# Softmax sums inverted on 16 columns by VectorE instead of 512, the context scaled by VectorE instead of GpSimd, and the score banks' two skipped places moved, in an attention layer on one core

## The chip, the cores and the metric

The kernel runs on one core of a Trainium2 chip. The metric is the device time in microseconds (us) of one execution, the median of several.

## The reference, cut to what matters

```python
x = L0_attn_query                      # 4 x 2048 x 512, fp32
xn = layernorm(x)
q, k, v = (split_heads(xn @ w.T + b) for each of q, k, v)       # 16 heads of 32
attn = softmax(q / sqrt(32) @ k.T)                              # per head 2048 x 2048
ctx = attn @ v
x + (ctx @ out_w.T + out_b) + tanh(((xn @ weight) @ aux1) @ aux2 + bias)
```

Four batches of 16 heads make 64 heads of attention, each with 2048 queries, 2048 keys and a head size of 32.

## The kernel before, in words

Three stages follow one another: `build_weights` prepares the weights, `build_project` makes q, k, v and the feed-forward part, and `build_attend` works through the 64 heads and then multiplies by the output weights. The change touches `build_attend` (and one constant in `build_weights`). Every order below is written out by hand; semaphores join the engines.

**TensorE.** A head has 64 units, 16 tiles of 128 keys (`kt`) by 4 blocks of 512 queries. For each unit TensorE makes two matmuls alternately: `scores` of the current head into one of three banks `st_bank` (line 1031), and `max_scores` (line 1015) of a head that comes later into one of four banks `sm_bank`, from which the row maxima are taken. They run in blocks of two tiles, 8 units, 16 matmuls. Behind each block stands `use` of the two tiles before (line 1037, `pv_bank`: probabilities times v). After tiles 8 and 9 of the next head comes `add_up`: the sum over the keys of the finished head, a matmul with `ones` that leaves each sum 32 times over in its bank `sum_bank`, which is one of the four `sm_bank` places.

**ScalarE** takes the exponential of each `st_bank` (line 846), copies `pv_bank` and the sums (line 853) to SBUF, and issues seven loads for a later head after tiles 6, 7, 9, 10, 12, 13 and 15 (lines 271 and 277).

**VectorE** reduces each `sm_bank` to its maxima (line 929), in the order of the units k = 0 to 63. Into this row the 512 reciprocals of the head's sums are put as three pieces (line 921), after k = 63, 7 and 15.

**GpSimd** adds ten of the sixteen probability tiles, nine instructions of 128x2048 (line 781, called add 0 to add 8 here). The other six tiles, `CHAINS`, are added by accumulating DMAs that GpSimd issues: join 1 to join 5 (line 792), each of which waits until the one before has landed, then `merge` (line 800), which adds GpSimd's sum and releases `add_up`. Its order per head is: join 1, add 0, merge of the head before, add 1, join 2, add 2, add 3, join 3, add 4, add 5, join 4, add 6, add 7, join 5, `scale` of the head before (line 806), add 8. Join 1 also waits for TensorE to have used tile 0 of its head, since tile 0 lies in the buffer that is added to.

**SyncE** stores each scaled context (line 700) and loads the row of maxima (line 695).

How a place of the three score banks is found:

```python
def st_slot(u):

    return u + (u >= 22) + (u >= 44)
```

A unit waits for the exponential of the last unit in the same bank. That is normally the third before it. After a skipped place two units wait for the second before, and one for the fifth before. Blocks begin at units that are multiples of 8.

Of the kernel before, what the change touches and what calls it, by code (L numbers as in the profile page):

```python
# [7 lines left out]
ACT = mybir.ActivationFunctionType  # L8
ALU = mybir.AluOpType
AX = mybir.AxisListType  # L10

P = 128
# [25 lines left out]
TURN_UNIT = 8  # L38
BEGIN = 16
SUM_UNIT = 56  # L40
RECIPS = [63, 7, 15]
CUT = 10
# [9 lines left out]
SLOT = {kt: i % 7 for i, kt in enumerate([*range(1, 13), 14, 15])} | {13: 7}  # L52
SCALE_ADD = 8
RESULT_TILES = [9, 11]
# [42 lines left out]
def st_slot(u):  # L97

    return u + (u >= 22) + (u >= 44)

# [9 lines left out]

assert early_maxima(BLOCKS - 1, BLOCK_UNITS - 1)[-1] == HEAD_MAXIMA - 1 and UNITS < TURN_SLOT
assert UNITS == 64 and len(SM_TURN) % SM_BANKS == 0 and st_slot(UNITS - 1) == 65


# [12 lines left out]
def build_weights(nc, x, w, dram, keep, first):  # L127

    with ExitStack() as own:
# [41 lines left out]
        @block.gpsimd  # L171
        def _(pool):
            nc.gpsimd.memset(keep["ident"][:], 0.0).then_inc(ident_ready, 1)
            nc.gpsimd.memset(keep["ones"][:], 1.0)
            nc.gpsimd.memset(keep["power"][:], -0.5)
            pool.wait_ge(ident_ready, 1)
            nc.gpsimd.affine_select(out=keep["ident"][:], in_=keep["ident"][:], compare_op=ALU.not_equal, fill=1.0,
                                    base=0, pattern=[[-1, P]], channel_multiplier=1).then_inc(ident_ready, 1)
            pool.wait_ge(var_ready, 1)
            nc.gpsimd.tensor_tensor(keep["rstd"][:], keep["rstd"][:], keep["power"][:], ALU.pow).then_inc(rstd_ready, 1)  # L180
# [426 lines left out]
def build_attend(nc, dram, out, first):  # L607
# [3 lines left out]
    with ExitStack() as own:  # L611
# [12 lines left out]
        pv_copy = [sb(f"pv_copy{s}", [P, BLK]) for s in range(2)]  # L624
        sum_copy = [sb(f"sum_copy{s}", [P, BLK]) for s in range(2)]
        ratio = sb("ratio", [P, BLK])
# [12 lines left out]
        join_due, joined = sem("join_due"), [sem("joined0"), sem("joined1")]  # L639
        pool_added, sums_ready, recip_ready, context_ready = sem("pool_added"), sem("sums_ready"), sem("recip_ready"), sem("context_ready")  # L640
        pv_copied, sums_copied = sem("pv_copied"), sem("sums_copied")
        context_stored = [sem("context_stored0"), sem("context_stored1")]
# [123 lines left out]
        def _(pool):  # L766
            pool.sem_inc(pool_added, PRIME)
            pool.sem_inc(context_ready, PRIME)
            nc.gpsimd.memset(k_st[3][MROW:MROW + 1, :].bitcast(F32), 1.0).then_inc(consts_ready, 1)
# [31 lines left out]

            def scale(h, r):
                pool.wait_ge(pv_copied, PRIME + h + 1)
                pool.wait_ge(recip_ready, h * len(RECIPS) + len(RECIPS))
                pool.wait_ge(context_stored[r % 2], PRIME + (h // 2) * (CTX_DMAS * DMA))
                nc.gpsimd.tensor_tensor(ctx_out[r % 2][:], pv_copy[r % 2][:], ratio[:], ALU.mult).then_inc(context_ready, 1)  # L806

            def sum_up(h, r, i):
# [21 lines left out]
        def _(act):  # L830
            for s in (probs_ready, pv_copied, sums_copied):
                act.sem_inc(s, PRIME)
# [16 lines left out]

            def copy_bank(h, r, bank, copies, ready, value, copied):  # L850
                act.wait_ge(ready, value)
                act.wait_ge(context_ready, PRIME + h - 1)
                nc.scalar.activation(copies[r % 2][:], bank[:], ACT.Copy).then_inc(copied, 1)  # L853

            def copy_pv(h, r):
                copy_bank(h, r, pv_bank, pv_copy, tile_used, PRIME + h * KT + KT, pv_copied)

            def copy_sums(h, r):
                copy_bank(h, r, sum_bank, sum_copy, sums_ready, PRIME + h + 1, sums_copied)

# [19 lines left out]
            def body(h, r, more, following):  # L880
                for kt in range(CUT, KT):
                    exps(h, r, kt)
                    if kt in LOAD_AT and more >= GROUP - 1:
                        load(h + GROUP - 1, (r + GROUP - 1) % GROUP, LOAD_AT.index(kt))
                if more:
                    for kt in range(CUT):
                        exps(following, (r + 1) % GROUP, kt)
                        if kt == 1:
                            copy_pv(h, r)
                        if kt in LOAD_AT and more >= GROUP:  # L890
                            load(h + GROUP, r, LOAD_AT.index(kt))
                        if kt == CUT - 1:
                            copy_sums(h, r)
                else:
                    copy_pv(h, r)
                    high(2, 0)
                    copy_sums(h, r)

# [5 lines left out]
        def _(dve):  # L904
            dve.sem_inc(max_scores_read, PRIME + UNITS + AHEAD * PER_TILE)
            dve.sem_inc(res_ready, PRIME)
            dve.sem_inc(row_max_ready, PRIME + 1)

            def negate(s):
# [3 lines left out]

            def recip(h, r, piece):

                if piece == 0:
                    dve.wait_ge(sums_copied, PRIME + h + 1)
                    dve.wait_ge(context_ready, PRIME + h)
                cut = [BLK // len(RECIPS) // 8 * 8 * i for i in range(len(RECIPS))] + [BLK]
                columns = slice(cut[piece], cut[piece + 1])  # L920
                nc.vector.reciprocal(ratio[:, columns], sum_copy[r % 2][:, columns]).then_inc(recip_ready, 1)  # L921
# [50 lines left out]
            def body(h, r, more, following):  # L972
                if more == 0:
# [7 lines left out]
                    results(1, 1)  # L981
                    for piece in range(len(RECIPS)):
                        recip(h, r, piece)
                else:
# [13 lines left out]
        def _(pe):  # L998
# [4 lines left out]
            def max_scores(s, r, k):  # L1003
# [182 lines left out]
```

## Time and profile before

| | us |
|---|---|
| median of 3 runs | 4139.67 (4138.31 to 4141.12) |
| profiled execution, its own time | 4140.99 |
| profiled execution, span | 4139.2 |
| TensorE busy | 4072.0 |
| VectorE busy | 3125.5 |
| ScalarE busy | 2356.7 |
| GpSimd busy | 3253.4 |

The span runs from the first to the last instruction of the profiled execution. TensorE's matmuls overlap, so its busy time holds waits too; start times are the better guide. The attention stage runs from about 0.82 ms to 3.98 ms.

### The profile page before, as it was taken

How to read it: one execution, taken by the hardware profiler on the slowest of the kernel's cores; microseconds unless marked ns; L12 is line 12 of the kernel's file. 1: busy time of each engine (PE TensorE's matmuls, PEld its weight loads, DVE VectorE, ACT ScalarE, POOL GpSimd, SP SyncE). 2: the span in 40 equal slices, each digit the busy share in tenths (PEclk: the TensorE clock that was granted, in tenths of full speed). 3: DMA queues.
4: the chain of work that ended last, by engine and by line, in shares of the span. 5: the costliest groups of instructions: out<-in, count | busy, mean ns of one | idle time of the engine just before them, and what ended most of it. 6: DMA issues, size and time to landing. Idle time of an engine off the chain costs nothing.

```text
span 4139.2 us, 77715 instructions
## 1 busy us (share of the span) xinstructions
PE 4072.0 (98%) x21216; PEld 2495.7 (60%) x21216; DVE 3125.5 (76%) x5058; ACT 2356.7 (57%) x4515; POOL 3253.4 (79%) x1180
## 2 busy tenths in 40 slices
PE   8999999999999999999999999999999999999999
PEld 6888888755555555555555555555555555555467
DVE  4344334788888888888888888888888888888554
ACT  2222222266666666766666667666666766676621
POOL 1222222299999999999999999999999999999930
PEclk9999999999999999999999999999999999999999
DMA  4444445578888888888888887888888888888787
GB/s 170 158 167 162 152 147 169 161 149 175 174 178 172 174 170 175 170 173 176 176 176 172 174 170 167 175 175 175 179 169 176 172 173 172 176 176 173 156 263 262
DMA packets 246352, 722.11 MB, mean 174 GB/s; under 512 B 87392, under 2 KB 88416, under 8 KB 184544
## 3 DMA queue, kind: packets, MB, share of 16 engines
q0 software_dynamic: 55296, 402.68, 50.2%
q1 hardware_dynamic: 107648, 201.88, 14.4%
q10 hardware_dynamic: 83040, 113.01, 9.8%
q8 instruction: 185, 3.03, 0.3%
q14 instruction: 183, 1.50, 0.1%
HBM read 178.00 MB, written 136.31 MB: 76 GB/s over the span
## 4 chain that ended last, share of the span: by engine, by line
PE 46%; DMA 19%; issue 9%; POOL 3%; ACT 3%; POOLq 0%; ACTq 0%; SPq 0%; DVE 0%; DVEq 0%
PE sm_bank L1015 14%; PE pv_bank L1037 14%; PE st_bank L1031 14%; DMA dma_sum<-probs 11%; DMA dma_sum<-pool_sum 8%; ACT probs L846 3%; PE sm_bank L261 2%; POOL pool_sum L781 2%; PE sm_bank L1037 1%; PE st_bank L261 1%; POOL ctx_out L806 1%; PE sm_bank L1024 0%; POOL dma_sum L792 0%; DMA q_stack<-s_ctx 0%; ACTq L845 0%
## 5 line engine op out<-in xcount | busy, mean ns | idle before, releaser
L929 DVE TENSOR_REDUCE part_max<-sm_bank 128x1 f32<-128x512 f32 x4016 | 2442.1, 678 | 410.9 <-PE sm_bank L1015 404.1
L781 POOL TENSOR_TENSOR pool_sum<-pool_sum,probs 128x2048 f32<-128x2048 f32 x512 | 2504.8, 4892 | 16.6 <-ACT probs L846 0.7
L846 ACT ACTIVATE probs<-st_bank 128x512 f32<-128x512 f32 x3840 | 1959.8, 616 | 611.9 <-PE st_bank L1031 585.5
L1031 PE MATMUL st_bank<-q_stack,k_stack 97*128 97x512 f32 x4096 | 1649.2, 404 | 15.0 <-ACT probs L846 8.5
L1015 PE MATMUL sm_bank<-k_stack,q_stack 96*128 96x512 f32 x4016 | 1655.5, 412 | 5.3 <-issue 2.8
L1015 PEld LDWEIGHTS sm_bank<-k_stack,q_stack 96*128 96x128 f32 x4016 | 764.8, 190 | 551.9 <-DVE part_max L929 331.7
L1031 PEld LDWEIGHTS st_bank<-q_stack,k_stack 97*128 97x128 f32 x4096 | 780.5, 191 | 268.4 <-ACT probs L846 127.5
L1037 PE MATMUL pv_bank<-probs,v_pairs 128*32 128x512 f32 x7680 | 934.9, 602 | 0.0
L1037 PEld LDWEIGHTS pv_bank<-probs,v_pairs 128*32 128x32 f32 x7680 | 205.5, 110 | 455.7 <-ACT probs L846 262.8
L792 POOL DMA_DIRECT2D dma_sum<-probs x320 | 348.6, 1089 | 66.0 <-ACT probs L846 28.9
L405 POOL TENSOR_TENSOR y_out<-y_out,x_in 128x512 f32<-128x512 f32 x64 | 82.8, 1293 | 369.6 <-ACT y_out L437 365.2
L781 POOL TENSOR_TENSOR pool_sum<-probs 128x2048 f32<-128x2048 f32 x64 | 330.5, 5164 | 0.1
L921 DVE RECIPROCAL ratio<-sum_copy 128x168 f32<-128x168 f32 (+1 forms) x192 | 230.9, 1204 | 38.1 <-ACT sum_copy L853 38.1
L524 DVE SCALAR_TENSOR_TENSOR qk_lo<-proj,qk_bias,qk_hi 128x512 fp32r<-128x512 f32 x128 | 96.1, 751 | 195.0 <-ACT qk_hi L431 193.3
L431 ACT ACTIVATE qk_hi<-proj,qk_bias 128x512 fp32r<-128x512 f32 x128 | 88.1, 688 | 272.4 <-PE proj L261 272.4
L437 ACT ACTIVATE y_out<-y_out 128x512 f32<-128x512 f32 x64 | 40.5, 632 | 319.6 <-DVE y_out L513 319.6
L846 ACT ACTIVATE dma_sum<-st_bank 128x512 f32<-128x512 f32 x256 | 132.4, 603 | 132.4 <-PE st_bank L1031 132.3
L394 POOL TENSOR_TENSOR rstd<-rstd,power 128x4 f32<-128x4 f32 x15 | 15.3, 1017 | 190.5 <-DVE rstd L459 190.5
L513 DVE TENSOR_TENSOR y_out<-proj,row_bias 128x512 f32<-128x512 f32 x64 | 44.3, 692 | 121.8 <-PE proj L261 121.8
L853 ACT ACTIVATE sum_copy<-sm_bank 128x512 f32<-128x512 f32 x64 | 38.2, 597 | 168.9 <-PE sm_bank L1037 168.9
L502 DVE TENSOR_TENSOR v_out<-proj,row_bias 128x512 f32<-128x512 f32 x64 | 44.3, 692 | 104.7 <-PE proj L261 104.7
L806 POOL TENSOR_TENSOR ctx_out<-pv_copy,ratio 128x512 f32<-128x512 f32 x64 | 103.6, 1619 | 20.8 <-issue 20.8
(116 smaller groups left out, 3198.6 us busy)
## 6 DMA issues: line engine op xcount, KB each, us to landing
dma_sum<-probs POOLq DMA_DIRECT2D x320, 1024.0 KB, 8.3
dma_sum<-pool_sum POOLq DMA_DIRECT2D x64, 1024.0 KB, 10.2
q_stack<-s_q_hi ACTq DMA_DIRECT2D x122, 256.0 KB, 6.4
k_stack<-s_k_hi ACTq DMA_DIRECT2D x122, 256.0 KB, 4.4
x_in<-in_x SPq DMA_DIRECT2D x16, 1024.0 KB, 7.7
s_q_hi<-qk_hi SPq DMA_DIRECT2D x16, 1024.0 KB, 4.3
s_q_lo<-qk_lo SPq DMA_DIRECT2D x16, 1024.0 KB, 6.4
s_k_hi<-qk_hi SPq DMA_DIRECT2D x16, 1024.0 KB, 4.3
```

What stands on the lines that cost most here:

```text
L261: last = nc.tensor.matmul(out, a(c), b(c), start=(c == 0 and n == 0), stop=(c == CT - 1 and n == 2))
L431: nc.scalar.activation(qk_hi[:, t, g], proj[:, u % RING], ACT.Identity, bias=keep["qk_bias"][:, t, g:g + 1]).then_inc(hi_ready, 1)
L524: nc.vector.scalar_tensor_tensor(qk_lo[:, t, g], proj[:, u % RING], keep["qk_bias"][:, t, g:g + 1], qk_hi[:, t, g].bitcast(F32), ALU.add, ...
L781: nc.gpsimd.tensor_tensor(total[:], one[:], tile_at(r, kt)[:], ALU.add).then_inc(pool_added, 1)
L792: nc.gpsimd.dma_start(dma_sum[r % 2][:], tile_at(r, CHAINS[0][j])[:], accum_op=ALU.add).then_inc(joined[r % 2], DMA)
L806: nc.gpsimd.tensor_tensor(ctx_out[r % 2][:], pv_copy[r % 2][:], ratio[:], ALU.mult).then_inc(context_ready, 1)
L846: nc.scalar.activation(tile_at(r, kt)[:, q * BLK:(q + 1) * BLK], st_bank[:, st_place(kt * QB + q)], ACT.Exp, scale=SCALE).then_inc(probs_r ...
L921: nc.vector.reciprocal(ratio[:, columns], sum_copy[r % 2][:, columns]).then_inc(recip_ready, 1)
L929: nc.vector.tensor_reduce(part_max[:, k:k + 1], sm_bank[:, sm_place(k)], AX.X, ALU.max).then_inc(max_scores_read, 1)
L1015: nc.tensor.matmul(sm_bank[:, sm_place(k)], q_st[r][0:ROWS, q * P:(q + 1) * P], k_st[r][0:ROWS, b * BLK:(b + 1) * BLK], start=True, stop=T ...
L1031: nc.tensor.matmul(st_bank[:, st_place(u)], k_st[r][0:ROWS + 1, kt * P:(kt + 1) * P], q_st[r][0:ROWS + 1, q * BLK:(q + 1) * BLK], start=Tr ...
L1037: last = nc.tensor.matmul(bank[q * DH:(q + 1) * DH, :], left, right[:, q * BLK:(q + 1) * BLK], start=start, stop=stop)
```

## The change

The sums' bank is read by VectorE with a reduction that transposes blocks of 32x32: of the 32 equal rows and 32 columns of a block it leaves one column, and 512 columns become 16. The 16 columns are inverted; since each sum is added 32 times, `ones` holds 1/32. A transposing copy spreads the 16 columns to 512 again, and VectorE, not GpSimd, multiplies the context. ScalarE's copy of the sums goes away; TensorE's next use of that bank waits for VectorE instead. The skipped places are at units 24 and 48.

```diff
+ST_SKIPS = (24, 48)
-RECIPS = [63, 7, 15]
+INVERT, SPREAD, SCALED = SUM_UNIT, 63, 15
...
-    return u + (u >= 22) + (u >= 44)
+    return u + sum(u >= skip for skip in ST_SKIPS)
...
-            nc.gpsimd.memset(keep["ones"][:], 1.0)
+            nc.gpsimd.memset(keep["ones"][:], 1.0 / DH)
...
-            def scale(h, r):
-                pool.wait_ge(pv_copied, PRIME + h + 1)
-                pool.wait_ge(recip_ready, h * len(RECIPS) + len(RECIPS))
-                pool.wait_ge(context_stored[r % 2], PRIME + (h // 2) * (CTX_DMAS * DMA))
-                nc.gpsimd.tensor_tensor(ctx_out[r % 2][:], pv_copy[r % 2][:], ratio[:], ALU.mult).then_inc(context_ready, 1)
...
-                    if i == SCALE_ADD:
-                        scale(h, r)
...
-                        if kt == CUT - 1:
-                            copy_sums(h, r)
...
+            def invert(h):
+                dve.wait_ge(sums_ready, PRIME + h + 1)
+                nc.vector.tensor_reduce(totals[:], sum_bank.rearrange("p (b j) -> p b j", j=DH), AX.X, ALU.add,
+                                        apply_transpose=True).then_inc(sums_turned, 1)
+                dve.wait_ge(sums_turned, PRIME + h + 1)
+                nc.vector.reciprocal(inverse[:], totals[:]).then_inc(inverse_ready, 1)
+
+            def spread_out(h):
+                dve.wait_ge(inverse_ready, h + 1)
+                nc.vector.transpose(ratio[:].rearrange("p (b j) -> p b j", j=DH),
+                                    inverse[:].unsqueeze(2).to_broadcast([P, BLK // DH, DH])).then_inc(ratio_ready, 1)
+
+            def scale(h, r):
+                dve.wait_ge(pv_copied, PRIME + h + 1)
+                dve.wait_ge(ratio_ready, h + 1)
+                dve.wait_ge(context_stored[r % 2], PRIME + (h // 2) * (CTX_DMAS * DMA))
+                nc.vector.tensor_tensor(ctx_out[r % 2][:], pv_copy[r % 2][:], ratio[:], ALU.mult).then_inc(context_ready, 1)
...
+                if k == INVERT and sums_of is not None:
+                    invert(sums_of[0])
                 if units:
...
-                if k in RECIPS and sums_of is not None:
-                    recip(*sums_of, RECIPS.index(k))
+                if k == SPREAD and sums_of is not None:
+                    spread_out(sums_of[0])
+                if k == SCALED and sums_of is not None:
+                    scale(*sums_of)
...
-                    pe.wait_ge(sums_copied, PRIME + s - 1)
+                    pe.wait_ge(sums_turned, PRIME + s - 1)
```

## Rows read from the trace of the kernel before

**Rows 1.** Waits from 1000 to 3900 us: total us, times, longest

```profile
PE sm_bank L1037 <- DMA dma_sum<-pool_sum: 24.1, 34, 2.5
```

**Rows 2.** Timeline of TensorE in one head: start, length, instruction, idle before

```profile
2002.18 1.07 PE L1037 MATMUL pv_bank<-dma_sum,v_pairs 128*32 128x512 f32 x8
...
2006.94 0.40 PE L1015 MATMUL sm_bank<-k_stack,q_stack 96*128 96x512 f32 x1
2007.41 0.50 PE L1031 MATMUL st_bank<-q_stack,k_stack 97*128 97x512 f32 x1
2007.74 0.39 PE L1015 MATMUL sm_bank<-k_stack,q_stack 96*128 96x512 f32 x1
...
2022.83 1.06 PE L1037 MATMUL sm_bank<-dma_sum,ones 128*32 128x512 f32 x8 [0.93 <-DMA dma_sum<-pool_sum]
...
2041.77 0.50 PE L1015 MATMUL sm_bank<-k_stack,q_stack 96*128 96x512 f32 x1
...
2051.58 1.07 PE L1037 MATMUL pv_bank<-dma_sum,v_pairs 128*32 128x512 f32 x8
```

**Rows 3.** Timeline of GpSimd in the same head: joins 1, 3, add 6, scale, add 8

```profile
2006.93 1.15 POOL L792 DMA_DIRECT2D dma_sum<-probs  x1
...
2029.23 0.88 POOL L792 DMA_DIRECT2D dma_sum<-probs  x1 [0.97 <-ACT probs L846]
...
2039.98 4.89 POOL L781 TENSOR_TENSOR pool_sum<-pool_sum,probs 128x2048 f32<-128x2048 f32 x1
...
2050.08 1.58 POOL L806 TENSOR_TENSOR ctx_out<-pv_copy,ratio 128x512 f32<-128x512 f32 x1
2051.34 4.86 POOL L781 TENSOR_TENSOR pool_sum<-pool_sum,probs 128x2048 f32<-128x2048 f32 x1
```

**Rows 4.** Timeline of VectorE in the same head, behind k = 63 and 15

```profile
2029.16 1.19 DVE L921 RECIPROCAL ratio<-sum_copy 128x168 f32<-128x168 f32 x1
...
2041.52 1.23 DVE L921 RECIPROCAL ratio<-sum_copy 128x176 f32<-128x176 f32 x1
2042.68 0.62 DVE L929 TENSOR_REDUCE part_max<-sm_bank 128x1 f32<-128x512 f32 x1
```

**Rows 5.** Issues of the merges, first and last start

```profile
L800 POOL DMA_DIRECT2D dma_sum<-pool_sum x64: 875/1494/1562, 886.7 to 3963.1; - x64
```

**Rows 6.** Timelines of VectorE and GpSimd near the end

```profile
3932.22 4.86 POOL L781 TENSOR_TENSOR pool_sum<-pool_sum,probs 128x2048 f32<-128x2048 f32 x1
...
3934.38 3.80 DVE L970 CAST q_stack<-q_stack 128x2048 fp32r<-128x2048 f32 x1 [2.98 <-DMA q_stack<-s_ctx]
3938.21 6.51 DVE L955 TENSOR_TENSOR k_stack<-q_stack 128x2048 fp32r<-128x2048 f32 x1
...
3937.22 5.35 POOL L781 TENSOR_TENSOR pool_sum<-pool_sum,probs 128x2048 f32<-128x2048 f32 x1
...
3969.37 2.29 DVE L955 TENSOR_TENSOR k_stack<-q_stack 128x2048 fp32r<-128x2048 f32 x1 [8.37 <-ACT q_stack L864]
```

**Rows 7.** Timelines of TensorE and GpSimd in the first full head

```profile
879.70 1.07 PE L1037 MATMUL pv_bank<-dma_sum,v_pairs 128*32 128x512 f32 x8
...
927.85 1.07 PE L1037 MATMUL pv_bank<-dma_sum,v_pairs 128*32 128x512 f32 x8
...
881.52 0.88 POOL L792 DMA_DIRECT2D dma_sum<-probs  x1 [4.18 <-PE pv_bank L1037]
...
904.70 0.89 POOL L792 DMA_DIRECT2D dma_sum<-probs  x1 [2.07 <-ACT probs L846]
...
915.46 4.86 POOL L781 TENSOR_TENSOR pool_sum<-pool_sum,probs 128x2048 f32<-128x2048 f32 x1
```

**Rows 8.** Timelines of TensorE and GpSimd in another head

```profile
1808.15 1.07 PE L1037 MATMUL pv_bank<-dma_sum,v_pairs 128*32 128x512 f32 x8
...
1810.92 1.15 POOL L792 DMA_DIRECT2D dma_sum<-probs  x1
...
1845.36 4.89 POOL L781 TENSOR_TENSOR pool_sum<-pool_sum,probs 128x2048 f32<-128x2048 f32 x1
```

More of the change, by code:

```diff
@@ L52 @@
 SLOT = {kt: i % 7 for i, kt in enumerate([*range(1, 13), 14, 15])} | {13: 7}
-SCALE_ADD = 8
 RESULT_TILES = [9, 11]
@@ L111 @@
 assert early_maxima(BLOCKS - 1, BLOCK_UNITS - 1)[-1] == HEAD_MAXIMA - 1 and UNITS < TURN_SLOT
+assert all(skip % (2 * PER_TILE) == 0 for skip in ST_SKIPS)
 assert UNITS == 64 and len(SM_TURN) % SM_BANKS == 0 and st_slot(UNITS - 1) == 65
@@ L624, in build_attend @@
         pv_copy = [sb(f"pv_copy{s}", [P, BLK]) for s in range(2)]
-        sum_copy = [sb(f"sum_copy{s}", [P, BLK]) for s in range(2)]
+        totals, inverse = sb("totals", [P, BLK // DH]), sb("inverse", [P, BLK // DH])
         ratio = sb("ratio", [P, BLK])
@@ L639, in build_attend @@
         join_due, joined = sem("join_due"), [sem("joined0"), sem("joined1")]
-        pool_added, sums_ready, recip_ready, context_ready = sem("pool_added"), sem("sums_ready"), sem("recip_ready"), sem("context_ready")
-        pv_copied, sums_copied = sem("pv_copied"), sem("sums_copied")
+        pool_added, sums_ready, context_ready = sem("pool_added"), sem("sums_ready"), sem("context_ready")
+        pv_copied, sums_turned = sem("pv_copied"), sem("sums_turned")
+        inverse_ready, ratio_ready = sem("inverse_ready"), sem("ratio_ready")
         context_stored = [sem("context_stored0"), sem("context_stored1")]
@@ L767, in _ @@
             pool.sem_inc(pool_added, PRIME)
-            pool.sem_inc(context_ready, PRIME)
             nc.gpsimd.memset(k_st[3][MROW:MROW + 1, :].bitcast(F32), 1.0).then_inc(consts_ready, 1)
@@ L830, in _ @@
         def _(act):
-            for s in (probs_ready, pv_copied, sums_copied):
+            for s in (probs_ready, pv_copied):
                 act.sem_inc(s, PRIME)
@@ L848, in exps, with copy_pv @@
                                          scale=SCALE).then_inc(probs_ready, 1)
-            def copy_bank(h, r, bank, copies, ready, value, copied):
-                act.wait_ge(ready, value)
+            def copy_pv(h, r):
+                act.wait_ge(tile_used, PRIME + h * KT + KT)
                 act.wait_ge(context_ready, PRIME + h - 1)
[L853 to L859, printed above, removed]
+                nc.scalar.activation(pv_copy[r % 2][:], pv_bank[:], ACT.Copy).then_inc(pv_copied, 1)
             def high(n, par):
@@ L896, in body @@
                     high(2, 0)
-                    copy_sums(h, r)
             heads(act, body)
@@ L907, in _ @@
             dve.sem_inc(row_max_ready, PRIME + 1)
+            dve.sem_inc(sums_turned, PRIME)
+            dve.sem_inc(context_ready, PRIME)
             def negate(s):
@@ L912, in negate @@
                                         ALU.mult).then_inc(max_row_ready, 1)
[L914 to L921, printed above, removed]
+            def invert(h):
[13 more added lines that the diff above has]
+                nc.vector.tensor_tensor(ctx_out[r % 2][:], pv_copy[r % 2][:], ratio[:], ALU.mult).then_inc(context_ready, 1)
             def maxima(s, k, units, sums_of):
+                if k == INVERT and sums_of is not None:
+                    invert(sums_of[0])
                 if units:
@@ L981, in body @@
                     results(1, 1)
-                    for piece in range(len(RECIPS)):
-                        recip(h, r, piece)
+                    invert(h)
+                    spread_out(h)
+                    scale(h, r)
                 else:
```

## The prediction

> **What bounds the kernel now.** I read the waits of the attention stage first. TensorE waits only in small pieces, most of it for the merge's DMA before `add_up` (24.1 us in 34 of some 60 heads [rows 1]). GpSimd, in the head read below, waits 0.97 us [rows 3]. So two engines run almost without a pause, and neither can gain alone. The merges are issued 3076.4 us apart over 63 heads [rows 5], so a head takes 48.83 us.
>
> Then I read one head on each engine. I count time in a head from U, the end of the first two-tile `pv_bank<-dma_sum` matmuls, when tile 0 has been used: U = 2003.25 here, and the next is 2052.65 [rows 2]. On TensorE the reader is to see three losses: 0.93 us idle before the sum matmul, and at a skipped place (unit 22, 2007.41) start gaps of 0.47 and 0.33 us where a plain pair has twice 0.235, so 0.33 lost [rows 2]. Unit 44 is the second such place. The shortest head runs from 880.77 to 928.92, 48.15 us [rows 7]; less two places at 0.33, TensorE's floor is 47.5 us.
>
> On GpSimd, join 1 starts at 2006.93, 3.68 us after U, so GpSimd lags behind what TensorE has ready. Join 3 waits 0.97 us. The row names ScalarE's exponential, but tile 8's had long been made; the join also waits for join 2 to land, and that came last. Add 6 ends at 2044.87; `scale` holds the queue for 1.26 us (2050.08 to 2051.34) [rows 3].
>
> **The change part by part.**
>
> *GpSimd* loses `scale`: 1.26 us per head [rows 3]. 48.83 less 1.26 is 47.57, beside TensorE's 47.5. This is the gain on offer.
>
> *The skipped places* move to the starts of blocks. Units 24 and 25 then wait for exponentials 22 and 23, which have the 1.85 us of a `use` to finish in. Both losses of 0.33 us should go. I give nothing back for them.
>
> *ScalarE* loses a copy of 0.6 us behind `add_up`. It has idle time; nothing but unit 44's place depended on it.
>
> *VectorE* loses three pieces (1.19 to 1.23 us each, 1.16 to the next start [rows 4]) and gains four instructions. The transposing sum and the spreading copy appear nowhere in the trace. Below, the 0.62 us of a plain reduction of 512 columns [rows 4] bounds them; above, the reciprocal's rate of about 7 ns a column, 3.6 us for 512. I take the former, the nearest in kind, for both; the reciprocal of 16 columns is about 0.2. Up to k = 15 that is 0.62 + 0.2 + 0.62 = 1.4 us against the 2.3 of the first two pieces. The sum stands ahead of k = 56, where it delays the next reductions by about 0.8, and the bank is given back in time if it stays near 0.62. I charge nothing, because of what follows: time ahead of k = 15 turns out to be covered by 2.9 us.
>
> *The multiplication on VectorE* decides. It reads two tiles in SBUF, `pv_copy` and `ratio`, while GpSimd adds tiles in SBUF nearly always. Near the end the trace has just such pairs [rows 6]. A cast asked for at 3934.38 stayed till 3938.18, which is 1.10 us after GpSimd's add ended at 3937.08. A subtraction of two SBUF tiles, asked for at 3938.21, stayed till 3944.72, 2.15 us after the next add's end at 3942.57. The same subtraction takes 2.29 us when GpSimd is quiet. So the VectorE instruction is held until GpSimd's running add ends, gets its turn before the next add, and that add is the longer for it (5.35 us). For 512 columns I take a quarter of 2.15 us, less the 0.07 by which the next instruction starts early: 0.5 us after the add's end. The Trainium skill, page "SBUF — State Buffer", section "Who interferes with whom", says the same in general: a VectorE instruction with two SBUF inputs and a GpSimd one that reads SBUF block each other, the later one until the first has finished; the trace agrees, 6.51 against 2.29 us.
>
> When is it asked for, and which add runs? The third piece starts at 2041.52, U + 38.3. Without 0.93 for the merge and 0.66 for the places it would be U + 36.7. Add 6 ends at U + 41.6 now [rows 3]. Relieved of `scale`, GpSimd runs ahead until join 1 meets its wait for tile 0. That wait is seen once, in the first full head: U = 880.77, join 1 at 881.52, so 0.75 us [rows 7]. From join 1 to the end of add 6 I have four values: 37.94 [rows 3]; 36.97 if its wait of 0.97 goes; 38.80 in the head with join 1 at U + 0.75 (881.52 to 920.32, with 2.07 us of wait at join 3 [rows 7]); 39.33 with join 1 at U + 1.70 (1810.92 to 1850.25 [rows 8]). The earlier the join, the longer the wait at join 3: the loads that ScalarE issues at fixed points of TensorE's course then fall into the merge and hold up join 2. I take 38.80, the head most like the new state, and keep 36.97 and 39.33 as bounds.
>
> So add 6 ends at U + 0.75 + 38.80 = U + 39.55, and the multiplication, asked for at U + 36.7, is held 2.9 us. Queued behind it is the reduction of unit 16. TensorE has four banks and can't start unit 20 before that one is read. Now unit 16's reduction starts at 2042.68; four of them, 0.61 us apart, end about 45.2, just when TensorE reaches unit 23 (unit 16 at 2041.77, its pair 0.57 long, then six of 0.47: 2045.2). There is no slack left, and each further microsecond is passed on. From 2042.68 to the next U is 9.97 us [rows 2, 4].
>
> The new chain closes on itself, head by head: 0.75 (U to join 1) + 38.80 (to the end of add 6) + 0.50 (multiplication) + 9.97 (unit 16's reduction to the next U) = 50.02 us. GpSimd's own course is shorter: 38.80, and from the end of add 6 to that of add 8 11.33 less 1.26, gives 48.9. So it does wait at join 1, as assumed. TensorE's 47.5 is shorter too, so that what the places and the merge's wait give back is lost again in the wait at unit 20, and the transposing sum costs nothing.
>
> 50.02 less 48.83 is 1.19 us per head. The last three heads have no loads beside them and take about 48.2; I count 60 heads: +71 us, less 2 for the last three, less 2 for what follows the last head (three pieces become about 2 us of VectorE, and a `scale` on GpSimd goes). +67 on the span of 4139.2 gives 4206. The profiled execution's own time is 4141.0 and the median 4139.7, so against the median the forecast is 4207 us, 1.6% slower. SyncE's store is released some 7 us earlier and lands in a quieter place; I count it at nothing, and if it fell into the merge it would add to the wait at join 3.
>
> **The rivals.**
>
> *It is not held* (faster). If 512 columns slip in between GpSimd's reads, the head takes 47.6 us, the larger of 47.5 and 47.57: 60 times 1.23 less, with the 4 above, 4062 us. For it speaks that only instructions of 2048 columns are seen held; against it that a cast and a subtraction both were, and the same subtraction beside a quiet GpSimd was not [rows 6]. It decides at a held time under 0.5 us.
>
> *The joins wait less* (about no change, or a little faster). With 37.94 the head takes 49.16, +0.33, so 4155 us; with 36.97 it takes 48.19, so 4097. For it: in the pinned state the fourth load falls just behind join 3. Against it: both heads with an early join 1 waited over 2 us.
>
> *The multiplication misses add 6 and is held by add 7.* That takes 2.9 us more of VectorE's time ahead of k = 15, and costs some 4.7 us per head: 54.7, or 4490 us. The spreading copy could bring it: if it is held like the cast, at k = 63 (U + 24.3, after the same 1.6) add 4 has just begun and lasts to about U + 29.4, 5 us, of which VectorE can make up about 1 us in each of the two blocks behind. By the same section of the Trainium skill an instruction with one SBUF input is held only in a two-port mode, which it lists for copy, cast and tensor_scalar; a transposing copy is not listed. By that the copy is free and my sum stands; by the cast's row it would come to the edge. No row here shows which.
>
> **How the numbers follow.** The chain as summed, with 38.4 to 39.5 (4180 to 4250 us), 0.52; joins that wait less but slower than before, 0.20; hardly any wait at join 3 (4097), 0.05; not held (4062), 0.13; held by add 7, 0.07; something that comes out as no change, 0.03. About 0.2% (8 us) is what a measurement of this kernel can tell from no change. So faster 0.20, same 0.06, slower 0.74. The bounds of the likeliest chain, 48.19 and 50.55 us a head, are 4097 and 4239 us. That range leaves out the first and the third rival, 2 in 10.
>
> **What would show it.** Right: the multiplication takes some 3 us and ends about 0.6 us after an add of GpSimd; GpSimd idles before join 1, waiting for `pv_bank`; join 1 starts at U + 0.75; the wait for the merge before the sum matmul is gone; TensorE waits for VectorE at unit 20 for about 2.5 us; heads take 50 us. Wrong: a multiplication of 0.7 us; join 1 still 3 us behind U; no 2 us of wait at join 3; or the transposing instructions over 2 us.

## The result, and the profile after

The changed kernel takes 4283.7 us (4281.3 to 4289.4, four runs), the one before 4140.4 us in the same comparison: a ratio of 1.0348, with a 95% interval of 1.0330 to 1.0366. It is 3.5% slower. The forecast was 4207 us in a range of 4097 to 4239, so the direction was right and the size was not.

The page of the profile after, its span and busy times:

```profile
span 4287.6 us, 77463 instructions
...
PE 4153.2 (97%) x21216; PEld 2518.9 (59%) x21216; DVE 3239.2 (76%) x5122; ACT 2336.1 (54%) x4451; POOL 3196.8 (75%) x1116
```

No engine has much more to do than before: VectorE is busy for 114 us more, in which the time that its multiplications are held counts as busy, and GpSimd for 57 us less. Yet the span grew by 148.4 us. The attention stage holds all of it: from the first to the last sum matmul it took 3076.7 us before and takes 3225.6 now, 148.9 more.

The new instructions, after, by the tiles that they write (shortest, median and longest in ns):

```profile
L902 DVE TRANSPOSE_TENSOR_REDUCE totals<-sm_bank x64: 716/717/718, 899.3 to 4125.8; 128x16 f32<-128x512 f32 x64
L905 DVE RECIPROCAL inverse<-totals x64: 252/253/255, 900.0 to 4126.6; 128x16 f32<-128x16 f32 x64
...
L909 DVE STREAM_TRANSPOSE ratio<-inverse x64: 696/698/712, 904.9 to 4126.8; 128x512 f32<-128x512 f32 x64
L916 DVE TENSOR_TENSOR ctx_out<-pv_copy,ratio x64: 693/3630/4734, 916.3 to 4127.6; 128x512 f32<-128x512 f32 x64
```

Three of them take the same time in all 64 heads. The multiplication takes 0.69 us when nothing is in its way, and 3.63 in the median.

The waits after, from 1000 to 4000 us (total us, times, longest):

```profile
POOL dma_sum L793 <- PE pv_bank L1037: 127.0, 57, 4.3
POOL dma_sum L793 <- ACT probs L839: 99.6, 58, 2.6
PE sm_bank L1015 <- DVE part_max L926: 94.5, 59, 2.8
```

GpSimd now waits for TensorE at join 1. The second line is join 3, which the view puts down to ScalarE's exponential; what comes last there is the landing of join 2 (see e7). TensorE waits for VectorE's reductions once per head. The merge's wait of [rows 1] is gone from the list. Now two heads on GpSimd (the first row of a head is its join 1; the `x2` behind join 4 are adds 6 and 7 in one row; alone, add 6 takes 4.86 us in both heads):

```profile
2007.25 0.88 POOL L793 DMA_DIRECT2D dma_sum<-probs  x1 [0.81 <-PE pv_bank L1037]
...
2029.33 0.89 POOL L793 DMA_DIRECT2D dma_sum<-probs  x1 [0.94 <-ACT probs L839]
...
2040.07 9.84 POOL L782 TENSOR_TENSOR pool_sum<-pool_sum,probs 128x2048 f32<-128x2048 f32 x2
...
2056.20 0.88 POOL L793 DMA_DIRECT2D dma_sum<-probs  x1 [0.82 <-PE pv_bank L1037]
...
2079.99 0.88 POOL L793 DMA_DIRECT2D dma_sum<-probs  x1 [2.62 <-ACT probs L839]
...
2090.76 9.83 POOL L782 TENSOR_TENSOR pool_sum<-pool_sum,probs 128x2048 f32<-128x2048 f32 x2
...
2109.23 0.88 POOL L793 DMA_DIRECT2D dma_sum<-probs  x1 [3.22 <-PE pv_bank L1037]
```

and the multiplication of each on VectorE, with the reductions behind it:

```profile
2042.80 2.69 DVE L916 TENSOR_TENSOR ctx_out<-pv_copy,ratio 128x512 f32<-128x512 f32 x1
2045.41 4.86 DVE L926 TENSOR_REDUCE part_max<-sm_bank 128x1 f32<-128x512 f32 x8
...
2091.72 4.47 DVE L916 TENSOR_TENSOR ctx_out<-pv_copy,ratio 128x512 f32<-128x512 f32 x1
2096.11 4.86 DVE L926 TENSOR_REDUCE part_max<-sm_bank 128x1 f32<-128x512 f32 x8
```

This is the mechanism of the forecast, to the tenth. In the first head add 6 ends at 2040.07 + 4.86 = 2044.93, and the multiplication at 2045.49. In the second, join 3 waits 2.62 us, add 6 ends at 2090.76 + 4.86 = 2095.62 and the multiplication at 2096.19. In all of 57 heads looked through, the multiplication ends 0.56 us behind add 6, and the next reduction starts up to 0.08 us before that. From unit 16's reduction to the next U (join 1 less 0.74) the first head takes 2045.41 to 2055.46: 10.05, where 9.97 had been taken. The second takes 2096.11 to 2108.49: 12.38. The same work, 2.4 us longer. TensorE in the second head shows why:

```profile
2093.92 0.39 PE L1031 MATMUL st_bank<-q_stack,k_stack 97*128 97x512 f32 x1
2096.84 0.80 PE L1015 MATMUL sm_bank<-k_stack,q_stack 96*128 96x512 f32 x1 [2.53 <-DVE part_max L926]
2097.44 0.63 PE L1031 MATMUL st_bank<-q_stack,k_stack 97*128 97x512 f32 x1
2097.86 0.63 PE L1015 MATMUL sm_bank<-k_stack,q_stack 96*128 96x512 f32 x1
...
2100.55 3.00 PE L1037 MATMUL pv_bank<-probs,v_pairs 128*32 128x512 f32 x16
2103.49 0.50 PE L1015 MATMUL sm_bank<-k_stack,q_stack 96*128 96x512 f32 x1
```

It stands still for 2.53 us at unit 20. The matmuls behind that start every 0.43 us instead of 0.235, and a `use` of 16 takes 3.00 us instead of 1.92. The windows of the same stretch (busy us of each engine, then the granted clock, the DMA share and GB/s) show it in the clock:

```profile
2091.00:2097.00 6.00, 3.47 (x21) 1.73 (x13) 6.00 (x5) 2.25 (x5) 5.92 (x3) 0.91 1.01 180
2097.00:2101.00 4.00, 4.00 (x12) 2.52 (x16) 3.97 (x7) 2.13 (x4) 4.00 (x2) 0.50 0.81 193
2101.00:2105.00 4.00, 4.00 (x22) 1.64 (x15) 0.98 (x2) 1.54 (x4) 4.00 (x2) 0.78 0.81 165
```

The granted clock was 0.50 from 2097 to 2101: TensorE ran at 1.2 and not 2.4 GHz, after it had stood still. Over the whole execution the granted clock is 0.5 for 231 us in 53 stretches; before it was so for 47 us in 12. Its mean is 0.973 against 0.995.

This head has one of the longer standstills. In 57 heads TensorE is idle ahead of unit 20 for 0.71 to 2.77 us, 1.6 on average. In the 42 heads in which the clock was then 0.5 for a time, it had been idle for 0.93 to 2.77 us (1.80 on average); in the other 15, for 0.71 to 2.12 us (1.07). So the longer standstill makes the fall likelier, but its length alone doesn't decide it.

Means per head, worked out from the traces (55 heads, from the fourth full one; us):

| | before | after |
|---|---|---|
| U to join 1 | 3.50 | 0.79 |
| join 1 to the end of add 6 | 37.77 | 38.51 |
| multiplication asked for, after U | – | 36.27 |
| held until add 6 ends | – | 3.02 |
| a head | 48.79 | 51.23 |

The chain of the forecast with its measured terms is 0.79 + 38.51 + 0.50 + 9.97 = 49.77. The head takes 51.23. So 1.46 us of each head stand outside the chain, 88 us over 60 heads, and the miss was 77.

To see whether these are the clock's, I set each head's excess over the chain beside the time for which the granted clock was 0.5 in that head. Of 57 heads, 15 have no such time, and their excess is 0.07 us on average and 0.08 at most. The other 42 have 4.5 us of it and an excess of 2.0 us. The correlation is 0.99.

### The profile page after: what moved, and what is told of

Same layout as the page of the kernel before. It is cut to its first block, busy times and chain, and to the rows that moved or that the text cites. A ratio compares the mean times of both kernels' runs of the same rounds, so it can differ in the third digit from the quotient of the medians.

```text
span 4287.6 us, 77463 instructions
## 1 busy us (share of the span) xinstructions
PE 4153.2 (97%) x21216; PEld 2518.9 (59%) x21216; DVE 3239.2 (76%) x5122; ACT 2336.1 (54%) x4451; POOL 3196.8 (75%) x1116
## 4 chain that ended last, share of the span: by engine, by line
PE 65%; issue 6%; DVE 6%; DMA 2%; POOL 1%; DVEq 0%; ACT 0%; ACTq 0%; POOLq 0%
PE sm_bank L1015 21%; PE pv_bank L1037 20%; PE st_bank L1031 18%; DVE part_max L926 5%; PE sm_bank L262 3%; DVE ctx_out L916 2%; PE sm_bank L1037 1%; DMA dma_sum<-probs 1%; PE st_bank L262 1%; POOL pool_sum L782 1%; DMA dma_sum<-pool_sum 0%; DVEq L925 0%; PE sm_bank L1024 0%; ACT probs L839 0%; DVEq L915 0%
## 5 line engine op out<-in xcount | busy, mean ns | idle before, releaser
L1015 PE MATMUL sm_bank<-k_stack,q_stack 96*128 96x512 f32 x4016 | 1697.3, 423 | 103.0 <-DVE part_max L926 98.0
L1037 PE MATMUL pv_bank<-probs,v_pairs 128*32 128x512 f32 x7680 | 985.3, 630 | 0.0
L1031 PEld LDWEIGHTS st_bank<-q_stack,k_stack 97*128 97x128 f32 x4096 | 790.4, 193 | 183.9 <-ACT probs L839 40.7
L793 POOL DMA_DIRECT2D dma_sum<-probs x320 | 322.4, 1008 | 262.5 <-PE pv_bank L1037 151.5
L782 POOL TENSOR_TENSOR pool_sum<-probs 128x2048 f32<-128x2048 f32 x64 | 313.4, 4897 | 0.1
L916 DVE TENSOR_TENSOR ctx_out<-pv_copy,ratio 128x512 f32<-128x512 f32 x64 | 224.9, 3514 | 0.2
L902 DVE TRANSPOSE_TENSOR_REDUCE totals<-sm_bank 128x16 f32<-128x512 f32 x64 | 45.9, 717 | 129.8 <-PE sm_bank L1037 129.8
L846 ACT ACTIVATE pv_copy<-pv_bank 128x512 f32<-128x512 f32 x64 | 38.3, 598 | 141.1 <-PE pv_bank L1037 141.1
```

What stands on the lines that cost most here:

```text
L782: nc.gpsimd.tensor_tensor(total[:], one[:], tile_at(r, kt)[:], ALU.add).then_inc(pool_added, 1)
L793: nc.gpsimd.dma_start(dma_sum[r % 2][:], tile_at(r, CHAINS[0][j])[:], accum_op=ALU.add).then_inc(joined[r % 2], DMA)
L916: nc.vector.tensor_tensor(ctx_out[r % 2][:], pv_copy[r % 2][:], ratio[:], ALU.mult).then_inc(context_ready, 1)
L1015: nc.tensor.matmul(sm_bank[:, sm_place(k)], q_st[r][0:ROWS, q * P:(q + 1) * P], k_st[r][0:ROWS, b * BLK:(b + 1) * BLK], start=True, stop=T ...
L1031: nc.tensor.matmul(st_bank[:, st_place(u)], k_st[r][0:ROWS + 1, kt * P:(kt + 1) * P], q_st[r][0:ROWS + 1, q * BLK:(q + 1) * BLK], start=Tr ...
L1037: last = nc.tensor.matmul(bank[q * DH:(q + 1) * DH, :], left, right[:, q * BLK:(q + 1) * BLK], start=start, stop=stop)
```

## The experiments

All but the last were planned on two questions: is the multiplication held by GpSimd's adds, and what is lost besides. "Of the changed kernel" names the kernel that an edit starts from.

| run | what it is | median us | ratio to before (95%) | head | at 1.2 GHz |
|---|---|---|---|---|---|
| before | | 4140.4 | 1 | 48.79 | 47 |
| after | the change | 4283.7 | 1.0348 (1.0330 to 1.0366) | 51.23 | 231 |
| e1 | multiplication back on GpSimd | 4165.5 | 1.0045 (1.0028 to 1.0063) | 49.07 | 96 |
| e2 | before, new places only | 4147.3 | 1.0009 (0.9994 to 1.0024) | 48.81 | 59 |
| e3 | one input, not two | 4090.6, one run | | 47.97 | 42 |
| e4 | ratio in PSUM | 4127.1 | 0.9964 (0.9950 to 0.9978) | 48.51 | 38 |
| e5 | multiplication behind k = 17 | 4189.1 | 1.0109 (1.0093 to 1.0126) | 49.53 | 113 |
| e6 | short adds on GpSimd | 4100.3, one run | | 48.36 | 23 |
| e7 | loads later | 4120.0 | 0.9941 (0.9925 to 0.9958) | 48.33 | 29 |
| e8 | ratio in PSUM, loads later | 4127.7 | 0.9957 (0.9941 to 0.9974) | 48.47 | 49 |
| e9 | before, loads later | 4106.9 | 0.9915 (0.9898 to 0.9931) | 48.26 | 34 |
| e10 | e1, loads later | 4108.7 | 0.9920 (0.9904 to 0.9937) | 48.23 | 34 |
| e11 | old places | 4234.4 | 1.0214 (1.0195 to 1.0233) | 50.46 | 141 |
| e12 | filled wait | 4207.0 | 1.0162 (1.0136 to 1.0189) | 49.82 | 42 |

Each ratio is to runs of the kernel before that were taken beside the run, with medians of 4140.4 to 4144.9 us. The last two columns come from the traces: mean us from one U to the next, and us in all with a granted clock of 0.5.

**e1, the multiplication back on GpSimd.** From the changed kernel:

```diff
+SCALE_ADD = 8
...
-                nc.vector.tensor_tensor(ctx_out[r % 2][:], pv_copy[r % 2][:], ratio[:], ALU.mult).then_inc(context_ready, 1)
+                nc.gpsimd.tensor_tensor(ctx_out[r % 2][:], pv_copy[r % 2][:], ratio[:], ALU.mult).then_inc(context_ready, 1)
...
             def spread_out(h):
+                dve.wait_ge(context_ready, PRIME + h)
```

> One part of the change undone: the multiplication goes back to GpSimd, in its old place before add 8; the transposing sum, the spreading copy on VectorE and the moved places stay. Theory (the held multiplication and the half clock that follows it are the whole loss; the rest of the change gains): no instruction of VectorE is held, no half clock in the middle of the heads, GpSimd is the bound with 47.9 us a head plus what join 3 waits, so 48.0 to 48.5 us a head and 4100 to 4120 us in all. Rival (the transposing sum, which stands in front of unit 56, or the later release of its bank costs TensorE something too): 4140 us or more.

Measured: 4165.5 us, 118 less than the changed kernel, so four fifths of the loss come with the multiplication's engine. But it is 0.45% slower than before, not faster. One line of its waits, 1000 to 4000 us:

```profile
PE sm_bank L1038 <- DMA dma_sum<-pool_sum: 63.8, 41, 4.2
```

Before, the same wait is 28.8 us in that stretch, and with the moved places alone (e2) it is already 47.6. So TensorE comes earlier to the merge's landing and waits there, and its clock is low for 96 us instead of 47. What the transposing sum frees on VectorE and ScalarE brought no gain here; e1 is even some 0.4% slower than e2, and why was not tried further than e10, where this goes.

**e2, the places alone.** In the kernel before:

```diff
-    return u + (u >= 22) + (u >= 44)
+    return u + (u >= 24) + (u >= 48)
```

> One part of the change alone: the kernel before with the skipped places at units 24 and 48. Theory: TensorE loses 0.66 us less per head, but GpSimd with its multiplication paces the heads with 47.9 us plus its waits at join 3, so that only a part comes through, 0.1 to 0.5 us a head: 4108 to 4134 us. Rival (TensorE paces the heads, GpSimd only follows): the full 0.66 us, 4098 us. Rival (all of it is lost in the wait for the merge): 4140 us.

Measured: 4147.3 us, a ratio of 1.0009 (0.9994 to 1.0024), no change; the last rival was right. TensorE's shortest head falls from 48.13 to 47.78 us, but its wait for the merge's landing grows from 28.8 us in 35 heads to 47.6 in 43 (1000 to 4000 us). The places' 0.66 us are not on the path that sets a head.

**e3, one input in SBUF and not two.** The multiplication becomes a transposing copy of `pv_copy` of the same size, so that the scaling is left out:

```diff
-                nc.vector.tensor_tensor(ctx_out[r % 2][:], pv_copy[r % 2][:], ratio[:], ALU.mult).then_inc(context_ready, 1)
+                nc.vector.transpose(ctx_out[r % 2][:], pv_copy[r % 2][:]).then_inc(context_ready, 1)
```

> The changed kernel with a transposing copy of pv_copy in place of the multiplication, at the same point of VectorE's order: the scaling is left out. It moves the same 512 columns, but has one input in SBUF, not two. Theory (two inputs in SBUF are what is held by GpSimd's add): it takes 0.7 us, no half clock, 47.6 us a head, 4065 us. Rival (whatever VectorE reads and writes in SBUF at this point is held, or the loss comes from the order of VectorE and not from the hold): again 3 us and 51 us a head, 4280 us.

Measured: 4090.6 us. Its instruction in that place is never held:

```profile
L916 DVE STREAM_TRANSPOSE ctx_out<-pv_copy x64: 690/698/711, 913.8 to 3929.8; 128x512 f32<-128x512 f32 x64
```

In 60 of the 64 heads it lies within one of GpSimd's adds. So this instruction, which reads one SBUF tile, passes while GpSimd adds, and the multiplication, which reads two, is held. That doesn't go for everything with one input: the cast of [rows 6] has one and was held. The Trainium skill, page "SBUF — State Buffer", section "Who interferes with whom", says that an instruction with at most one SBUF input outside the two-port modes doesn't contend with GpSimd; the trace agrees for the transposing copy, 698 against 3630 ns.

**e4, the ratio in PSUM.** The spreading copy writes into a free place of the four `sm_bank` banks and the multiplication follows at once, so that it reads one tile in SBUF and one in PSUM:

```diff
-INVERT, SPREAD, SCALED = SUM_UNIT, 63, 15
+INVERT, SPREAD, SCALED = SUM_UNIT, 63, 63
...
-SM_TURN = [..., *range(SUM_UNIT, UNITS), None, None]
+SM_TURN = [..., *range(SUM_UNIT, UNITS), "ratio", None]
...
-        ratio = sb("ratio", [P, BLK])
+        ratio = sm_bank[:, sm_place("ratio")]
...
```

> The change kept whole, multiplication on VectorE, but the spread ratios lie in PSUM, in the bank of the free place behind unit 63, and the multiplication follows at once behind unit 63. It then has one input in SBUF and one in PSUM. TensorE's unit 2 of the next row waits for it. Theory: not held, 0.7 us; GpSimd keeps its 1.26 us, the heads take TensorE's 47.5 to 47.9 us: 4060 to 4085 us. Rival (GpSimd's own course with its waits at join 3 takes over): 48.5 us a head, 4120 us. Rival (held all the same): 4280 us.

Measured: 4127.1 us, 0.36% faster than before.

```profile
L916 DVE TENSOR_TENSOR ctx_out<-pv_copy,sm_bank x64: 686/687/690, 907.3 to 3964.7; 128x512 f32<-128x512 f32 x64
```

The same multiplication with an operand in PSUM takes 686 to 690 ns in all 64 heads, in 58 of them within one of GpSimd's adds. With e3 this shows that the hold of the multiplication is bound to its second SBUF input, not to the instruction or to its place.

The time is that of the first rival, but not for its reason. The median head, 48.47 us, is hardly longer than the shortest, 48.43, and that is longer than the 47.50 of e3's shortest. TensorE's block behind the ratio's bank, in which it makes `max_scores` for units 0 to 7 of the next row, takes 4.82 us on average and 3.94 in e3; the other seven blocks differ from e3's by less than 0.1 us. So the bank that the ratio occupies costs TensorE 0.9 us a head.

**e5, the multiplication behind k = 17.** Asked for 2.2 us later (at U + 38.48 on average), with add 6 still running:

```diff
-BEGIN = 16
+BEGIN = 20
...
-INVERT, SPREAD, SCALED = SUM_UNIT, 63, 15
+INVERT, SPREAD, SCALED = SUM_UNIT, 63, 17
...
```

> The changed kernel with its multiplication behind k = 17 in place of k = 15. It is asked for about U + 38.2 instead of U + 36.3, still before add 6 ends (U + 38.4 at the earliest), and two more reductions stand ahead of it, so that TensorE can go two units further. Theory (a chain through the end of add 6, plus half clock when TensorE stands still for 2 to 3 us): held about 2 us less 1.9 where add 6 ends as before, TensorE waits some 1 us less, no or little half clock, 48.2 to 48.9 us a head: 4105 to 4150 us. Rival (the request now often comes after add 6 and is held by add 7): a multiplication of 4 to 5 us in part of the heads and more than 4280 us. Rival (the loss does not hang on the place): 4280 us.

Measured: 4189.1 us. The direction was as expected, the size not: a hold shorter by 1.9 us and two reductions done before it give 1.7 us a head, but the clock is still low for 113 us.

**e6, short adds.** All adds of GpSimd but the first of a head are cut to 64 columns, which leaves 1984 of 2048 columns of the sums out:

```diff
+                n = SEQ if i == 0 else 64
-                nc.gpsimd.tensor_tensor(total[:], one[:], tile_at(r, kt)[:], ALU.add).then_inc(pool_added, 1)
+                nc.gpsimd.tensor_tensor(total[:, 0:n], one[:, 0:n], tile_at(r, kt)[:, 0:n], ALU.add).then_inc(pool_added, 1)
```

> The changed kernel with GpSimd's adds 1 to 8 on 64 columns instead of 2048: most of the sum over the keys is left out. The joins, the merge and all the rest stay. Theory (only a running add of GpSimd holds the multiplication): 0.7 us for it, no half clock in the heads, and heads at TensorE's own pace with the places moved, 47.5 us: 4058 us. Rival (VectorE's order or the transposing instructions cost TensorE time by themselves): 48.5 us a head or more, 4120 us and up.

Measured: 4100.3 us. Without the adds the multiplication takes 0.68 us with both tiles in SBUF. Neither this kernel nor e3 reaches the 4062 us of the forecast's first rival: the mean head is 48.36 us here and 47.97 in e3. The shortest heads are 47.46 and 47.50 us, and the median here is 47.55, so TensorE's own pace is the 47.5 of the forecast. What lengthens the mean is waits in some of the heads (1000 to 3900 us): in e3 15.0 us in 23 heads for the merge's landing, here 26.9 us in 24 for the load of the row of maxima.

**e7, the loads later.** Of ScalarE's seven loads three leave the stretch between the merge and join 3. It issues four there in a head of the changed kernel and one in e7, and this one after join 2 has landed:

```diff
-LOAD_AT = [6, 7, 9, 10, 12, 13, 15]
+LOAD_AT = [2, 10, 11, 12, 13, 14, 15]
```

> The changed kernel with ScalarE's seven loads behind tiles 2 and 10 to 15 instead of 6, 7, 9, 10, 12, 13 and 15, so that none is issued between the merge and the landing of join 2. Theory (loads that fall into the merge hold up join 2, so join 3 waits, so add 6 ends late, so the multiplication is held long, so TensorE stands still long enough for half clock): join 3 waits under 0.5 us, join 1 to the end of add 6 takes 37.0 to 37.4 us and not 38.5, the multiplication about 2 us and not 3.6, half clock goes, 48.2 to 48.8 us a head: 4100 to 4140 us. Rival (join 3's wait is the time of merge and join 2 alone, whatever the loads): unchanged, 4280 us.

Measured: 4120.0 us, 164 less than the changed kernel. From 1000 to 4000 us its waits at join 3 and at unit 20 are nearly gone:

```profile
PE sm_bank L1015 <- DVE part_max L926: 14.6, 18, 1.6
...
POOL dma_sum L793 <- ACT probs L839: 11.1, 15, 1.4
```

Join 2 lands 8.4 us after its issue on average, where it took 12.0 in the changed kernel. Add 6 now ends 36.92 us behind join 1. The chain gives 0.79 + 36.92 + 0.50 + 9.97 = 48.18, and a head takes 48.33; of 55 heads all but one are 0.10 to 0.15 us above their chain. So the sum of the forecast holds when its terms are moved, as long as TensorE hardly stands still. The multiplication is still held: it takes 1.8 us in the median.

**e8, the ratio in PSUM and the loads later.** e4 with e7's line (and the second free place of the banks).

> The ratios in PSUM as before, but in the bank of the second free place, so that unit 3 and not unit 2 waits for the multiplication (0.47 us later), and the loads late. Theory: unit 2's wait of 0.36 us goes, GpSimd's course is 46.7 us plus a small wait, TensorE's 47.7 to 48.0: 4070 to 4090 us. Rival (the loads do not matter): GpSimd's course stays 48.5 and the time 4127 us.

Measured: 4127.7 us, not as expected and no better than e4: a head takes 48.47 us. GpSimd's wait at join 3 is gone, but the block behind the ratio's bank still takes 4.87 us instead of 3.94. The ratio in a bank sets TensorE's pace at 48.4 us, whichever of the two free places it takes.

**e9, the loads later in the kernel before.** e7's line alone, in the kernel before.

> The kernel before with the loads behind tiles 2 and 10 to 15, and nothing else. Theory: join 3's wait of 0.8 us goes, GpSimd's course falls from 48.8 to 47.9 us a head, TensorE has 48.1 with the old places, so 48.1 to 48.3 us a head: 4095 to 4110 us. Rival (the loads mattered only to the changed kernel, whose join 1 comes early): 4140 us.

Measured: 4106.9 us, 0.85% faster than before. The median head, 48.23 us, is within 0.1 of the shortest, 48.14, which is TensorE's own pace with the old places.

**e10, the loads later in e1.** e7's line in the kernel of e1.

> Multiplication on GpSimd, the transposing sum and the moved places kept, loads late. Theory: GpSimd's course is 46.7 + 1.26 = 47.9 us, TensorE's 47.5: 47.9 to 48.1 us a head, no half clock in the heads, 4085 to 4100 us, some 20 us under the changed kernel with late loads, which is held 2 us. Rival (the longer heads with multiplication on GpSimd came from something other than the loads): 4165 us as before.

Measured: 4108.7 us, 57 less than e1, and the same as e9 within both intervals. So e1's loss was made with the loads in the merge's stretch. And once they are out of it, the inversion on 16 columns and the moved places give nothing that can be measured; the shortest head is 47.50 us, but the mean is 48.23.

**e11, the old places in the changed kernel.**

```diff
-ST_SKIPS = (24, 48)
+ST_SKIPS = (22, 44)
```

> The changed kernel with the skipped places back at units 22 and 44. Theory (the chain through the end of add 6 sets the head and covers everything that TensorE loses ahead of unit 20's wait): the same time within 0.3%, 4275 to 4295 us, and the multiplication held about 0.6 us less. Rival (TensorE's losses count as well): 0.66 us a head more, 4325 us.

Measured: 4234.4 us, 49 less than the changed kernel, where no difference had been expected. TensorE reaches the multiplication's point later, so VectorE asks for it later and it takes 0.6 us less (2.97 on average), as expected. What had not been: TensorE stands still less at unit 20 (60.5 us from 1000 to 4000 us, not 94.5), and the time at 1.2 GHz falls from 231 to 141 us. The chain is 0.79 + 38.32 + 0.50 + 9.97 = 49.58 us and the head 50.46. The excess over the chain is 0.88 instead of 1.46, 35 of the 49 us; the chain, shorter by 0.19, is 11 more.

**e12, the wait filled with matmuls.** So far the clock's part rested on a correlation. Here TensorE repeats one matmul six times ahead of unit 20's wait:

```diff
+                for n in range(7 if u == 3 else 1):
-                nc.tensor.matmul(st_bank[:, st_place(u)], ...).then_inc(scores_ready, 1)
+                    last = nc.tensor.matmul(st_bank[:, st_place(u)], ...)
+                last.then_inc(scores_ready, 1)
```

> The changed kernel, in which TensorE repeats the score matmul of unit 3 six more times (same place, same operands, same values) before it goes on to unit 20's wait, so that some 1.4 us in which it now stands still are filled with matmuls whose results change nothing. GpSimd, VectorE, ScalarE and the DMA queues keep their work. Theory (the 1.46 us a head by which the changed kernel exceeds its chain of 49.77 us is matmuls run at 1.2 GHz after TensorE has stood still): the chain stays, the stretches with granted clock 0.5 fall from 231 us to under 100, a head takes 49.8 to 50.2 us, and the whole 4195 to 4225 us, although TensorE does more. Rival A (the excess is something else, and TensorE has slack): about 4284 us. Rival B (TensorE has no slack, and the repeats add to its course): up to 1.4 us a head more, 4300 to 4370 us.

Measured: 4207.0 us (4205.6 to 4217.3), 77 less than the changed kernel, with 384 more matmuls. A head takes 49.82 us, and the terms of the chain are those of after (0.79, and 38.46 from join 1 to add 6). The granted clock is 0.5 for 42 us instead of 231. TensorE in a head in which the multiplication took 4.12 us, almost as long as the 4.47 shown above:

```profile
2116.81 1.76 PE L1032 MATMUL st_bank<-q_stack,k_stack 97*128 97x512 f32 x7
2119.37 0.50 PE L1015 MATMUL sm_bank<-k_stack,q_stack 96*128 96x512 f32 x1 [0.80 <-DVE part_max L926]
2119.71 0.40 PE L1032 MATMUL st_bank<-q_stack,k_stack 97*128 97x512 f32 x1
2119.97 0.51 PE L1015 MATMUL sm_bank<-k_stack,q_stack 96*128 96x512 f32 x1
...
2121.83 1.92 PE L1038 MATMUL pv_bank<-probs,v_pairs 128*32 128x512 f32 x16
```

It still waits for the same reduction, but only 0.80 us are empty (from 1000 to 4000 us such waits are 20.5 us in all, not 94.5). Behind it the matmuls start every 0.30 us, VectorE's pace, and the `use` takes 1.92 us, not 3.00. Of 55 heads one is still 2.96 us above its chain, the only one in which the clock falls; the other 54 are 0.04 to 0.27 us above it. Both rivals are out: the excess was the clock.

## Why the prediction was wrong

**Right: the mechanism and its terms.** Join 1 starts 0.79 us behind U (0.75 forecast). The multiplication is asked for at U + 36.27 (36.7), is held 3.02 us (2.9) until add 6 ends, and the next reduction starts 0.5 us behind it. The merge's wait went, TensorE waits for VectorE at unit 20, GpSimd for TensorE at join 1, and join 3 waits longer. From join 1 to the end of add 6 it is 38.51 us (38.80), which alone would have made the forecast 0.29 x 60 = 17 us less. The transposing instructions took 0.72 and 0.70 us where I had taken the 0.62 of a reduction; their cost lies where there was slack. The question that the forecast left open, whether the spreading copy is held like the cast, is answered: in 52 of 64 heads it lies within an add and takes 0.70 us all the same. One reading was wrong, at no cost to the sum: the 5.35 us of GpSimd's add [rows 6] are not the price of VectorE's turn. Adds 1 and 2 take 5.38 and 5.35 us on average over the heads of the kernel before, with no such instruction beside them. What the turn costs GpSimd shows in add 7, 4.89 us against 4.59.

**The step that failed: "There is no slack left, and each further microsecond is passed on. From 2042.68 to the next U is 9.97 us."** It passes each microsecond on once, and takes the work behind the wait at the pace that it had before. But behind TensorE's standstill at unit 20 (1.6 us on average) its granted clock falls to 0.5 in 42 of 57 heads, and part of these 9.97 us is done at 1.2 GHz. 9.97 became 11.43 on average. That is 1.46 us a head, 88 us in 60 heads, less 15 for the chain's own terms (49.77 and not 50.02): 4207 + 73 = 4280, beside the measured 4284. e12 gives the other side. With the clock held up, the kernel with nearly the same chain takes 4207.0 us. That this is the forecast's number to the microsecond is partly luck, since e12's chain is 0.3 us a head shorter than mine.

**It could have been read.** The trace of before has one head of 52 us. The windows of that head (granted clock third from the end) and TensorE's timeline show the same fall, behind the wait for a merge:

```profile
1740.00:1779.00 39.00, 36.45 (x208) 20.16 (x201) 31.50 (x52) 25.03 (x49) 38.46 (x14) 1.00 0.86 179
1779.00:1783.00 4.00, 4.00 (x13) 2.87 (x10) 2.66 (x4) 2.54 (x5) 3.97 (x1) 0.58 0.83 172
```

```profile
1778.31 1.07 PE L1037 MATMUL sm_bank<-dma_sum,ones 128*32 128x512 f32 x8 [2.48 <-DMA dma_sum<-pool_sum]
...
1780.47 0.63 PE L1031 MATMUL st_bank<-q_stack,k_stack 97*128 97x512 f32 x1
1780.90 0.63 PE L1015 MATMUL sm_bank<-k_stack,q_stack 96*128 96x512 f32 x1
```

A wait of 2.48 us there, and matmuls every 0.43 us behind it. [rows 1] listed the longest such wait as 2.5 us, and the forecast put a wait "for about 2.5 us" into every head (it came out as 1.6 on average). The two belonged together.

**Wrong in size: what was on offer.** The forecast had a head of 47.5 us if the multiplication was not held, 4062 us. Without the hold e3 gives 47.97 and 4090.6; e4 and e8 give 48.5. With the multiplication left on GpSimd (e1) the rest of the change makes the kernel 0.45% slower. TensorE's floor of 47.5 was right: the shortest heads of e1, e3, e6 and e10 take 47.46 to 47.51. But a mean head lies above the floor by what the engines wait for landings, of the joins, of the merge and of the row of maxima, and the comparison of 47.57 and 47.5 left these out. In e4 and e8 the bank of the ratio lifts the floor itself. No run takes the merge's wait out of e3, so how much of its 0.47 us that wait makes stays open.

**Wrong: "what the places and the merge's wait give back is lost again", at no cost.** In the kernel before, the places are worth nothing (e2). In the changed kernel they cost 49 us (e11): time won ahead of a wait makes the wait longer, and the longer standstill costs clock. In e11 TensorE's wait at unit 20 is 1.1 us on average, in the changed kernel 1.6.

**Right in kind: join 3.** The loads that fall into the merge's stretch were named as what makes join 3 wait. e7 shows it, with 1.6 us a head less between join 1 and add 6; and e9 that the same line is worth 0.85% in the kernel before. e9 is the fastest version that computes the whole result, and beats both kernels. Of the change itself nothing is worth keeping beside it: e10 is level with e9, and e7, with the multiplication on VectorE, is 13 us slower, with intervals that overlap a little.

## What to carry to other kernels

When a change puts a wait of 1 to 3 us into TensorE's course, don't pass it on one to one: find the longest standstills of TensorE in the trace before, and read the granted clock and the spacing of the matmuls behind them. Here that added 1.46 us to a stall that was otherwise worth some 1 us.

Before an elementwise operation moves from GpSimd to VectorE, count its SBUF inputs and ask which of GpSimd's instructions runs at that moment. With one operand in PSUM, or with a transposing copy in its place, 3.6 us became 0.7. Count what the PSUM bank costs as well: here it was 0.9 us of TensorE's time a head. And look at what is issued beside a chain of accumulating DMAs before tuning the engines: moving three loads out of it won 0.85% in the kernel before, and 164 us in the changed one.

## What the runs showed of the hardware that was not expected

- TensorE's granted clock fell to 0.5 behind single standstills of 0.93 to 2.77 us, with the engine busy nearly all the rest of a 50-us head. Not every one brought it: after 2.12 us in the changed kernel, and 3.51 us in e1, a head kept its full clock. 53 stretches made 231 us at 1.2 GHz, and a head lost 0.44 us for each microsecond of them (1.46 by 3.35).
- Matmuls whose results change nothing won 77 us of 4284, since they kept the clock up.
- A held VectorE instruction gets its turn between two adds that GpSimd has back to back: the 64 multiplications of 0.69 us took 0.69 to 4.73, and in each of 57 heads the end came 0.56 us behind add 6, before add 7 was done.
- Plain loads that ScalarE issues lengthen GpSimd's accumulating DMAs beside them: join 2 took 12.0 us to land with four loads issued between the merge and join 3, and 8.4 with three of them moved (after, e7).
